# Mixture-of-experts decoder: the router inside cross attention, ten groups' rows scattered early, and the hand-off between the two attentions interleaved

## What is computed

```
def _L0_ffn_ref(x, W1, W2, Wr):
    logits = jnp.einsum('btd,ed->bte', x, Wr)
    probs = jax.nn.softmax(logits / TEMPERATURE, axis=-1)
    topk_vals, topk_idx = jax.lax.top_k(probs, TOPK)
    router_weights = topk_vals / topk_vals.sum(-1, keepdims=True)
    one_hot = jax.nn.one_hot(topk_idx, E, dtype=x.dtype)
    gate = jnp.einsum('btk,btke->bte', router_weights, one_hot)
    h = jax.nn.silu(jnp.einsum('btd,efd->btef', x, W1))
    y = jnp.einsum('btef,edf->bted', h, W2)
    out = jnp.einsum('bte,bted->btd', gate, y)
x = _layernorm(x + _L0_attn_ref(...))    # 8 heads, blocks of 64
x = _layernorm(x + _L0_xattn_ref(...))   # 16 heads, keys and values from a context
x = _layernorm(x + _L0_ffn_ref(...))     # 8 experts, two per token
```

## Time and profile before

| what | us |
|---|---|
| median of 3 runs | 1191.63 (1186.92 to 1197.12) |
| profiled execution | 1183.26 |
| its span, first to last instruction | 1181.5 |
| TensorE busy in the span | 916.7 (78%) |
| VectorE busy | 835.4 (71%) |
| ScalarE busy | 714.1 (60%) |
| GpSimd busy | 417.0 (35%) |

### The profile page before, as it was taken

The page is one execution under the profiler, slowest core; times in us unless marked ns, Lnnn a source line. Parts: engine busy times, 40 slices in busy tenths (PEclk is TensorE's granted clock), DMA queues, the critical chain, the costliest instruction groups (busy, mean ns, idle before and its releaser), DMA issues. The chain is left out here.

```text
span 1181.5 us, 30674 instructions
## 1 busy us (share of the span) xinstructions
PE 916.7 (78%) x11050; PEld 818.3 (69%) x11051; DVE 835.4 (71%) x2501; ACT 714.1 (60%) x1192; POOL 417.0 (35%) x473
## 2 busy tenths in 40 slices
PE   3888887888669999999999999720006999999991
PEld 2677777777548888888888888510006999999991
DVE  3587887878748888888888888484003777777772
ACT  3666766666358766777667774410003888888881
POOL 3142432424310100000100000514772677777774
PEclk9898988988779999999999999555557999999996
DMA  5920000000010000000010000000113333232220
GB/s 166 214 57 19 18 9 18 12 15 18 1 23 13 12 22 13 12 11 11 11 22 11 0 1 1 1 0 27 53 53 62 65 75 63 64 72 65 65 50 1
DMA packets 103714, 42.09 MB, mean 36 GB/s; under 512 B 58290, under 2 KB 99516, under 8 KB 103668
## 3 DMA queue, kind: packets, MB, share of 16 engines
q1 hardware_dynamic: 98676, 32.93, 13.4%
q0 software_dynamic: 4992, 8.54, 2.3%
HBM read 20.66 MB, written 16.57 MB: 32 GB/s over the span
## 5 line engine op out<-in xcount | busy, mean ns | idle before, releaser
L453 PE MATMUL psum<-XTa,qz 128*128 128x128 f16 x768 | 146.2, 226 | 38.5 <-ACT XTa L773 38.5
L962 DVE TENSOR_TENSOR at<-psum,rc 64x32 f32<-64x32 f32 (+1 forms) x768 | 153.2, 200 | 14.4
L787 ACT ACTIVATE pr<-psum 128x512 f32<-128x512 f32 x192 | 114.1, 594 | 79.1 <-PE psum L532 77.9
L946 DVE TENSOR_REDUCE mx<-psum 128x8 bf16<-128x512 f32 x192 | 132.8, 692 | 29.4 <-PE psum L455 23.8
L791 ACT ACTIVATE pt<-psum 128x512 f32<-128x512 f32 x192 | 113.3, 590 | 61.2 <-PE psum L541 60.9
L455 PE MATMUL psum<-XTa,qz 128*128 128x128 f16 x768 | 146.8, 227 | 0.0
L454 PE MATMUL psum<-XTa,qz 128*128 128x128 f16 x768 | 146.7, 227 | 0.0
L431 POOL DMA_INDIRECT out_dram<-X,dest x92 | 123.9, 1346 | 61.0 <-ACT X L855 42.9
L453 PE MATMUL psum<-cth,W 128*128 128x128 f16 x384 | 69.0, 223 | 85.5 <-DMA cth<-xd 85.5
L1129 DVE TENSOR_TENSOR qkl<-pr,qkh 128x1024 f16<-128x1024 f32 x46 | 56.4, 1226 | 107.8 <-ACT pr L864 107.8
L863 ACT ACTIVATE qkh<-psum 128x1024 f16<-128x1024 f32 x46 | 46.8, 1018 | 139.7 <-PE psum L455 139.7
(11 more groups left out here) (196 smaller groups left out, 2891.3 us busy)
## 6 DMA issues: line engine op xcount, KB each, us to landing
xd<-blank SPq DMA_DIRECT2D x1, 6072.0 KB, 35.2
X<-xd SPq DMA_DIRECT2D x23, 264.0 KB, 2.9
X<-x_dram SPq DMA_DIRECT2D x16, 256.0 KB, 2.9
wst<-w_dram SPq DMA_DIRECT2D x16, 256.0 KB, 2.8
cin<-ctx_in_dram SPq DMA_DIRECT2D x16, 256.0 KB, 2.8
out_dram<-X,dest POOLq DMA_INDIRECT x92, 2.9
mraw<-mask_dram SPq DMA_DIRECT2D x32, 32.0 KB, 2.5
xd<-XTa,pos POOLq DMA_INDIRECT x64, 2.3
```

The source lines that it names most:

```text
L453: nc.tensor.matmul(out_, lh, rh, start=start, stop=False, **kw)
L787: nc.scalar.activation(pr[u % 2][:], SC[u % 2][:], ACT.Exp).then_inc(s["ex"], 1)
L946: nc.vector.tensor_reduce(mx[u % 2][:], SC[u % 2][:].rearrange("p (r k) -> p r k", k=S), AX.X, ALU.max).then_inc(s["mx"], 1)
L962: m = nc.vector.tensor_tensor(dst, src, r, ALU.mult)
```

## The change

**Router in the bodies.** From cross group 2 on, the body of group g also does the router of group g - 2: ScalarE copies the high rows (high_rows, slot 1) and the high part of the transposed tokens (rh, slot 4), TensorE transposes (RT, slot 4) and makes logits (slot 6, written into a free part of a values bank), VectorE takes the low part (rl, slot 4) and copies the logits (keep, slot 6). At the end of each odd body VectorE runs select for a pair of groups, and GpSimd then adds up running sums over eight tiles (running). In each even body from 4 on TensorE ranks the pair before (rank, slot 2) and VectorE reduces the result (of_class in slot 2, own_rank in slot 3). Four bodies at each end are written out, and the loop holds 4 to 11.

**Early scatter.** In group 12 VectorE also computes the gates of the first ten groups, the capacity that their classes need, and the places of their 40 tiles. The rows of the six groups after get places in what room is left and in blocks behind it. GpSimd issues the 40 scatters in groups 12 to 15, in the numbers of SENT_BEFORE and SENT_AFTER (before and after the inverse deviation), and 24 at the end.

**Hand-off.** Cross attention's opening is interleaved with the end of self attention: transposes, projections and masked copies of q for group 0, and between them the last values, output projection and layer norm of self group 15. The masked copies of k of cross attention move to another buffer (wst), which the weight pieces occupied; so they wait for the last split. The memory of the router's tables moves too, and the softmax over all eight experts is replaced by the exponential of the difference between the two best logits.

```diff
...
+        def over_groups(la, eng, body):
+            edge = 4 if la.cross else 2
+            for g in range(edge):
+                body(g, g % 2, min(2, G - 1 - g), g // 2)
+            with eng.Fori(edge // 2, (G - edge) // 2) as j:
+                body(2 * j, 0, 2, j)
+                body(2 * j + 1, 1, 2, j)
+            for g in range(G - edge, G):
+                body(g, g % 2, min(2, G - 1 - g), g // 2)
...
+            def low_rows(h):
+                wait_apart(pool, r_hr, h + 1, pool_ready, POOL_READY)
+                nc.gpsimd.tensor_tensor(xhl[:, tiles_of(h), D:2 * D], X[:, tiles_of(h), :], xhl[:, tiles_of(h), 0:D], ALU.subtract).then_inc(r_lr, 1)
...
+                    late = la.cross and isinstance(g, int) and g >= GA + 2
+                    if route:
+                        low_rows(g - 2)
                     if follow >= 2:
                         ahead(g + 2, i)
+                    if late:
+                        send(SENT_BEFORE[g])
+                    if not la.cross and follow == 0:
+                        next_opening()
                     if not first_group(g):
                         inv_std(g - 1, s["mv"], before, s["rs"])
+                    if late and g == GA + 2:
+                        pool.wait_ge(r_lr, GA)
+                        pool.wait_ge(r_id, 1)
+                        pool.wait_ge(cleared, 16)
+                        pool.wait_ge(r_pos, 2)
+                    if late:
+                        send(SENT_AFTER[g])
+                    if route and i == 1:
+                        running(p - 1)
...
+            next_opening, next_groups = attention(CROSS, G, None)
+            opening, groups = attention(SELF, 0, next_opening)
+            opening()
+            groups()
             pool.wait_ge(sems["self"]["fin"], G)
-            attention(CROSS, G)
-            pool.wait_ge(sems["cross"]["fin"], G)
             nc.gpsimd.iota(token, pattern=[[P, NT], [0, 2]], base=0, channel_multiplier=1).then_inc(r_id, 1)
...
-            for g in range(G):
-                ts = slice(g * GT, (g + 1) * GT)
-                pool.wait_ge(r_hr, g + 1)
-                nc.gpsimd.tensor_tensor(xhl[:, ts, D:2 * D], X[:, ts, :], xhl[:, ts, 0:D], ALU.subtract).then_inc(r_lr, 1)
+            next_groups()
+            for h in range(G - 2, G):
+                low_rows(h)
             pool.wait_ge(r_lr, G)
-            pool.wait_ge(r_id, 1)
-            pool.wait_ge(r_pos, 1)
-            pool.wait_ge(cleared, 16)
-            for t in range(NT):
-                if t % SEG == 0 and t >= 2 * SEG:
-                    pool.wait_ge(sent[t // SEG - 2], 16 * SEG)
-                nc.gpsimd.indirect_dma_start(out=xd, out_offset=bass.IndirectOffsetOnAxis(ap=pos[:, t:t + 1], axis=0),
-                                             in_=rows_out[:, t, :], in_offset=None).then_inc(sent[t // SEG], 16)
+            pool.wait_ge(r_pos, 4)
+            send(range(GA * GT, NT))
...
+                def RT(h, vh):
+                    pe.wait_ge(s["fin"], h + 1)
+                    pe.wait_ge(s["vh"], vh)
+                    wait(pe, r_xl, h)
+                    if isinstance(h, int):
+                        for t in range(GT):
+                            m = nc.tensor.transpose(M0[:, t * P:(t + 1) * P], X[:, h * GT + t, :], ident[:])
...
+                def opening(last_values, last_out):
+                    XT(0, 0)
+                    if la.cross:
+                        pe.wait_ge(sems["self"]["zz"], G - 1)
+                        CT(0, 0)
+                        last_values()
+                    Qp(0, 0)
+                    Kp(0, 0)
+                    Vp(0, 0)
+                    if la.cross:
+                        pe.wait_ge(s["klo"], 1)
+                        last_out()
+                    XT(1, 1)
+                    if la.cross:
+                        pe.wait_ge(sems["self"]["zz"], G)
+                        CT(1, 1)
+                    scores(0, 0, 0)
+                    scores(0, 1, 0)
+                    less_max(0, 0)
...
+                    if la.cross:
+                        last_out()
+                        vh(0, 0)
+                        act.wait_ge(w_split, G)
+                    for part in of_k:
...
+                        if ranked and u == slot(la, "RANK"):
+                            dve.wait_ge(s["pv"], g * la.nh + u)
+                            of_class(p - 2, lead)
+                            if tables:
+                                whole(lead)
+                        if route and u == slot(la, "LG"):
+                            dve.wait_ge(s["pv"], g * la.nh + u)
+                            keep(g - 2, i, p - 1, lead)
...
+                        if tables and u == 1:
+                            gates_of(0)
+                        if ranked and u == slot(la, "OWN"):
+                            own_rank(p - 2)
+                            if tables:
+                                capacity(0)
+                        if tables and u == slot(la, "OWN") + 1:
+                            place_rows(0, 0)
+                        if tables and u == slot(la, "OWN") + 2:
+                            place_rows(0, 1)
+                        if route and u == slot(la, "RT"):
+                            rl(g - 2)
...
+                    if route and i == 1:
+                        select(p - 1)
...
+                    rl(G - 2)
+                    last["norm"]()
+                    last["al"]()
+                    last["stats"]()
+                    of_class(NPAIR - 2, last_rk[0])
+                    own_rank(NPAIR - 2)
+                    keep(G - 2, 0, NPAIR - 1, last_lg[0])
+                    last["finish"]()
+                    rl(G - 1)
+                    keep(G - 1, 1, NPAIR - 1, last_lg[1])
+                    select(NPAIR - 1)
+                    running_on(NPAIR - 1)
+                    gates_of(1)
+                    of_class(NPAIR - 1, last_rk[1])
+                    whole(last_rk[1])
+                    own_rank(NPAIR - 1)
+                    capacity(1)
+                    place_rows(1, 0)
+                    place_rows(1, 1)
+                    words()
...
+                then(nc.vector.tensor_reduce(best, LG, AX.X, ALU.max))
+                then(nc.vector.tensor_tensor(same, LG, each(best), ALU.is_equal))
+                then(nc.vector.tensor_tensor(same, same, low_index, ALU.mult))
+                then(nc.vector.tensor_reduce(first, same, AX.X, ALU.min))
+                then(nc.vector.tensor_tensor(same, low_index, each(first), ALU.is_equal))
+                then(nc.vector.scalar_tensor_tensor(out=left, in0=same, scalar=-BIG, in1=LG, op0=ALU.mult, op1=ALU.add))
+                then(nc.vector.tensor_reduce(next_best, left, AX.X, ALU.max))
+                then(nc.vector.tensor_tensor(gap[:, tiles_of_pair(p)], next_best, best, ALU.subtract))
+                then(nc.vector.tensor_tensor(same, left, each(next_best), ALU.is_equal))
+                then(nc.vector.tensor_tensor(same, same, low_index, ALU.mult))
+                then(nc.vector.tensor_reduce(second, same, AX.X, ALU.min))
+                then(nc.vector.tensor_tensor(turned[:, tiles_of_pair(p)], first, second, ALU.is_gt))
+                then(nc.vector.tensor_tensor(lesser, first, second, ALU.min))
+                then(nc.vector.tensor_tensor(both, first, second, ALU.add))
+                then(nc.vector.scalar_tensor_tensor(out=key, in0=lesser, scalar=float(E - 1), in1=both, op0=ALU.mult, op1=ALU.add))
+                then(nc.vector.tensor_tensor(M16[:, tiles_of_pair(p), :], key.unsqueeze(2).to_broadcast([P, PT, NP]),
+                                             code.unsqueeze(1).to_broadcast([P, PT, NP]), ALU.is_equal), True)
...
+SENT_BEFORE = {12: range(0), 13: range(4, 12), 14: range(15, 24), 15: range(28, 37)}
+SENT_AFTER = {12: range(0, 4), 13: range(12, 15), 14: range(24, 28), 15: range(37, 40)}
 SLOTS = {"self": {"QK": 0, "V": 1, "AT": 1, "O": 2, "XT": 3},
-         "cross": {"QK": 0, "V": 2, "AT": 3, "O": 4, "XT": 5, "CT": 6}}
+         "cross": {"QK": 0, "V": 2, "AT": 3, "O": 4, "XT": 5, "CT": 6, "HIGH": 1, "RANK": 2, "OWN": 3, "RT": 4, "LG": 6}}
...
```

More of the change, by code:

```diff
@@ L34 @@
 SEG = 16
[L35 removed]
+NX = 24 + P + 3 * NP + 2 + NJ
 class Layer:
@@ L464, in XT @@
                     wait(pe, s["vh"], g)
+                    if la.cross:
+                        wait(pe, r_xl, g - 3)
                     for t in range(GT):
@@ L659, in _ @@
+                return opening, lambda: over_groups(la, pe, body), closing if la.cross else (last_values, last_out)
+            pe.wait_ge(prep, PREP)
+            opening, groups, last = attention(SELF)
+            opening(None, None)
+            groups()
+            opening, groups, closing = attention(CROSS)
+            opening(*last)
+            groups()
+            closing()
             pe.wait_ge(r_lot, 1)
```

(25 more changed lines are left out.)

506 lines of the change are left out of this document (297 added, 209 removed).

## The result

The changed kernel takes **1172.97 us** (median of 4 runs, 1172.04 to 1175.13) against 1190.19 us in the same measurement: ratio 0.985, 95% interval 0.982 to 0.988. The forecast was 1145, so it is faster by 17 us where 47 were forecast, though inside the range. The profiled execution has a span of 1173.3 us.

What follows compares the result with a forecast made beforehand. Bound by TensorE (94% busy) and VectorE (86%) in cross attention, plus 143 us serial behind it. Gains of 107.7 us less losses of 61 net -46.7: 1183.3 to 1136.6, or 1145 us in the runs' measure; range 1105 to 1180.

Steps and rivals of the forecast that it cites:

- Step 1: Serial scatters behind cross attention: 40 of them issued during groups 12 to 15 take 50.7 us off the tail.
- Step 2: Router chain from last normalisation to first scatter: 62.0 us before, 18.0 after, so 44.0 us go.
- Step 3: Hand-off from self to cross attention: the first row maximum comes 13 us earlier (5 to 16).
- Step 4: Cross attention loop pays for the router: 6.0 us a pair, 42 us for seven, plus 5 in group 12.
- The second rival: Cross attention loop: TensorE's clock falls at each selection, six more falls of 3 us, 18 in all, 1163 us; chance 20%.
- Step 5: Scatters in groups 13 to 15: VectorE's normalisation waits some 9 us in group 13; groups 14 and 15 lose 2 together.
- The clock after the stall of group 13: Cross attention group 13: the 9 us stall lowers TensorE's granted clock once, costing 3 us.
- VectorE's idle time: Cross attention loop: idle time takes the router's work, so the loop pays 13 us instead of 42; 1116 us; chance 22%.
- Slow scatters, the third: Groups 13 to 15: scatters beside VectorE work take up to 2.09 us each, adding 20 us; 1165 us; chance 10%.

## Why the prediction was right and wrong

- **Step 1, scatters behind the last group:** right. 50.7 us by the run with all late, 50.7 forecast.
- **Step 2, tail chain:** nearly right. 19.65 us from the end of the last normalisation (824.63) to the first late scatter, 18.0 forecast. The row places took 5.7 us and not 4.9, and from the last of them to the first scatter another 0.8 us pass, which the sum left out; the selection in it, 4.0 us, was nearly right.
- **Step 3, hand-off:** right. Last softmax copy to first maximum in 18.7 us instead of 32.0, 13.3 gained, 13 forecast.
- **Step 4, the loop:** the mechanism was right, its terms too small. Without scatters the loop costs 60.7 us (420.0 against 359.3 in the second profile of before) where the prediction had 42 + 5 = 47. Its parts:
  - the router's other work is 1.7 us a group, read where no selection stands (26.77 against 25.05), forecast 1.3;
  - the selection is 4.3 us of VectorE, not 3.8, and costs a pair 58.1 - 53.5 = 4.6, not 3.4. "After a selection TensorE would idle 2 us, work and idle 1.3 again; I leave full clock in the forecast and the fall to a rival" is the sentence that failed: it idles 2.46 us and the clock falls each time. The second rival had this, at 3 us a fall; the windows show up to 2.2, and some 0.8 in the mean, so most of the 4.6 is VectorE's time and not the clock;
  - the tables of group 12 cost 38.65 - 30.5 = 8 us, forecast 5. This one is read from the intervals alone; no run took it apart.
- **Step 5, scatters in the loop:** this step failed. Group 13's wait was right (9 forecast, 8.40 waited, 8.5 us given back by the run without them). Groups 14 and 15 were counted at 2 us, since GpSimd has time for the scatters there; they cost 16.4. The step asked only what is queued behind the scatters on GpSimd. That they might delay TensorE's signals to engines that wait for nothing of GpSimd's was put at nothing, without a reason.
- **The clock after the stall of group 13:** 3 us forecast; no run tells it from the rest.
- **The rivals:** VectorE's idle time did not absorb the work (pairs of 58.1, not 52). Slow scatters, the third, fall: scatters in the loop are 1.26 to 1.28 us apart (only the second of a row comes 1.29 to 1.55 us after the first), behind it 1.26 to 1.27 (1.40). The rule of the Trainium skill ("SBUF — State Buffer", section "SBUF: two separate sides"), by which they would be slowed by VectorE's copies, does not show in the loop: the scatter at 749.57, beside VectorE's masked copies (L1083), took 0.99 us against 0.96 behind the loop. The output scatters of the feed-forward stage do take up to 2.04 us beside VectorE work, in the kernel before up to 1.80; the prediction says that the trace of before has its scatters where VectorE rests, but that holds for the router's 64 alone. What lengthens the others was not taken apart. In the loop, what suffered were TensorE's signals.

In sum: scatters in the loop 11.2 us more than forecast (25.2 against 9 + 2 + 3), the router's work in it 13.7 more by the run without scatters (60.7 against 47), 2.4 more in the profile after, and the tail 1.7: 29 of the 30 us by which the effect fell short.

## What to carry to other kernels

Moving a serial chain of small dependent instructions under a dense stage does not make it free: on VectorE, at 86% here, it cost TensorE four fifths of its time, and a fall of the clock at every block. Putting each instruction between two independent ones took the price of a selection from 4.6 to 2.2 us. When DMA descriptors are issued from an engine with idle time, look at the other engines' waits too. Here rows of at most three with pauses between them, in front of GpSimd's long waits rather than behind them, were best. Profile the kernel before twice before charging a stage's growth to the change.

## What was not expected of the hardware

- While GpSimd issues indirect DMAs in a row (1.27 us each), signals from TensorE to VectorE and ScalarE come late. In every kernel that had rows of four or more beside attention there were waits that the profile marks "remote"; the latest signal came 8.7 us behind its matmuls (the early scatters behind the inverse deviation: transposes ended at 724.56, copy at 733.22). With 26 scatters in rows of three at most no wait had the mark, as with none at all. With 36 there was one in a row of three, of 3.57 us. The mechanism is open, and so is the share of the instruction loads; the feed-forward stage also issues its scatters beside other work, and whether its 285 or 294 us have to do with this was not tried.
- The feed-forward stage of one and the same kernel took 285.0 us in one execution and 294.4 in another (windows above), at the same mean clock.
- The same instructions took 28.7 to 28.9 or 31.1 us, by whether TensorE's granted clock had a mean of 0.95 and more or of 0.89 in the interval.
